# The expert mixture of a fused adaLN block: one fp32 matmul replaced by two fp32r matmuls over split operands

## The chip, the cores and the metric

One Trainium2 chip, one of its cores. The metric is the time of one execution on the device in microseconds (us), the median of several runs. An execution uses five engines that run their own instruction streams and wait for one another by semaphores: PE (TensorE, matmuls), ACT (ScalarE), DVE (VectorE), POOL (GpSimd) and SP (SyncE, which here only issues DMAs).

## The reference

A transformer block with adaptive layer norm, on x of 4 x 512 tokens and 512 features. Its first half is causal attention with 32 heads of 128 (8 key/value heads). Its second half, which the change is in, is a router over 64 experts whose experts are only bias rows:

```
h = _layernorm(x) * (1 + cb) + sb
logits = einsum('th,eh->te', flat, router_weight) + router_bias
scores = softmax(logits)
topk_w, topk_idx = top_k(scores, 8)
w_sum = topk_w.sum(axis=-1, keepdims=True)
w_dense = zeros((T, 64)).at[arange(T)[:, None], topk_idx].add(topk_w)
out = flat * w_sum + einsum('te,eh->th', w_dense, expert_bias)
x = x + gb * out
```

The last einsum is the mixture: for each tile of 128 tokens, a [128 x 64] matrix of weights times the [64 x 512] matrix of expert rows.

## The kernel before, in words

The attention runs as 128 head steps, `t` = 0 to 127. Four steps (h = `t % 4` = 0 to 3, the heads of one key/value group) make a unit `u`, which is one group of one batch row; the units of the first three batch rows come first. Each engine has a `step(t)` of its own in which its work stands in a fixed order written by hand, and the engines meet only through semaphores. Nearly every large matmul of the attention is of the split type: an operand is held as a high part, which ACT makes by copying to fp32r, and a low part, which POOL or DVE makes by subtracting the high part from the original; three fp32r passes (lo x hi, hi x lo, hi x hi) add up in PSUM.

The second half works on 16 tiles of 128 tokens. Tiles 0 to 11 (the first three batch rows) are woven into the steps from `FFN_FROM` = 91 on, one stage of the pipeline in every second step: `ffn_tile(t)` gives n for t = 91, 93, 95, ..., 121, and in that step the engines do for tile n-1 norm, transpose and copy, for n-2 the logits and bias, for n-3 exp, top-8 and weights, and for n-4 the mixture and output. So the weights of tiles 0 to 11 are made in steps 97, 99, ..., 119, and their mixtures in steps 99 to 121. The last four tiles a, b, c, d come after the attention, in the tail, in an order of their own.

Order of a step with an n, as far as the change touches it:

- PE: scores of step t+1, q projection of t+3 (`q_proj`, L467), k or v projection, output projection of t-2 (L564), **mixture of tile n-4** (`ffn_mix`, L596), logits of n-2 (L584), values of t-1 (L549), transpose of h2 for n-1 (L575), **transpose of the weights of n-3** (`ffn_weights_T`, L591). The score matmuls of the next step follow in the queue.
- ACT: `exponentials`, `normalise`, `q_split` (L777: the high part of q for step t+3, which waits for POOL's `rot_c`, L1393), then h2T copy (L830) and **weightT copy** (L844).
- DVE: `ffn_norm`, `q_rope`, `ffn_top` of n-3 (L1186 to L1209, of which L1201 is the `tensor_tensor` of `ffn_choose`), bias of n-2 (L1173), `ffn_out` of n-4 (L1223), then `transpose_blocks(t+1)` (L1088), in steps with h = 1 two `add_out` (L1104), and then, at the head of the next step, `mask_and_max` (L1063 and L1065), which reads the bank of scores `s3` that the next `q_proj` writes.
- POOL: `split_moved_lo` (L1404), `ffn_norm` (L1450, L1452), `q_rope` (L1393), `q_split` (L1398: the low part of q, released by ACT's L777), in h = 0 `k_rope`, then `ffn_out` (L1458, L1460), and in the steps between those with an n also `ffn_stats` and `ffn_gate` (L1426).

PE's queue is strictly in order. `q_proj(t)` begins with `pe.wait_ge(dve_s, score_read(t - 2, 3))`: it may not write bank `s3` before DVE has read the scores of step t-2 out of it.

Of the kernel before, what the change touches and what calls it, by code (L numbers as in the profile page):

```python
# [7 lines left out]
F32 = mybir.dt.float32  # L8
# [106 lines left out]
def build(nc, A, out):  # L115
    ctx = ExitStack()
    with ctx:
# [35 lines left out]
        for at, p in ((wq_at, "hi"), (wq_at + 4 * GROUP * CH * HD, "lo")):  # L153
# [42 lines left out]
        experts = after0.take("experts", [EXPERTS, HID])  # L196
        router = after0.take("router", [P, CH, EXPERTS])
        logit, rest, weight = ([after0.take(f"{n}{i}", [P, EXPERTS]) for i in range(W_RING)]
                               for n in ("logit", "rest", "weight"))
        weightT = [after0.take(f"weightT{i}", [EXPERTS, P]) for i in range(W_RING)]  # L200
# [3 lines left out]
        h2 = [(after1 if i < F_RING - 1 else after2).take(f"h2_{i}", [P, HID]) for i in range(F_RING)]  # L204
        gate1, shift2, scale2, gate2 = [], [], [], []
# [107 lines left out]
        def sem(name):  # L313
# [16 lines left out]
        d_xin, d_xend, d_router = sem("d_xin"), sem("d_xend"), sem("d_router")  # L330
# [32 lines left out]
         out_done) = (sem(f"f_{n}") for n in (  # L363
             "gated", "residual", "x1", "stat", "aggregated", "with_eps", "root", "normed", "scaled", "shifted", "transposed",
             "h2T", "logits", "bias", "minus_max", "exp", "top", "replaced", "chosen", "weighed", "wT", "wT_copy",
             "mix", "mixed", "gated2", "out"))
# [39 lines left out]
        def tensor_program(pe):  # L406
# [172 lines left out]
            def ffn_logits(i, ps):  # L579
                if 0 <= i < TILES:  # L580
                    pe.wait_ge(h2T_copy, i + 1)
                    pe.wait_ge(d_router, 48)
# [141 lines left out]
        def scalar_program(act):  # L724
# [114 lines left out]
            def ffn_weights_copy(i, ps):  # L839
                if 0 <= i < TILES:  # L840
# [3 lines left out]
                    act.activation(weightT[i % W_RING][:], bank[ps][0:EXPERTS, 0:P], ACT.Copy).then_inc(wT_copy, 1)  # L844

            def step(t):
# [98 lines left out]
            ffn_h2T(c, "pv")  # L945
            ffn_weights_copy(a, "s1")
            ffn_exp(b)
            ffn_h2T(d, "pv")
            ffn_weights_copy(b, "s1")
            ffn_exp(c)  # L950
            ffn_weights_copy(c, "s1")
            ffn_exp(d)
            ffn_weights_copy(d, "s1")


        def vector_program(dve):
# [209 lines left out]
            def ffn_bias(i, ps):  # L1166
                if 0 <= i < TILES:
# [4 lines left out]
                    dve.wait_ge(d_router, 48)  # L1172
# [16 lines left out]
            def ffn_replace(i):  # L1189
                if 0 <= i < TILES:  # L1190
                    w = i % W_RING
                    dve.wait_ge(top_done, i + 1)
                    if i >= W_RING:
                        dve.wait_ge(weighed, i - W_RING + 1)
# [8 lines left out]
            def ffn_weigh(i):  # L1203
                if 0 <= i < TILES:
                    s, w = small[i % F_RING], i % W_RING
                    dve.wait_ge(chosen, i + 1)
                    if i >= W_RING:
# [599 lines left out]
```

## Time and profile before

| | |
|---|---|
| median of 3 runs | 1544.13 us (1540.83 to 1544.83) |
| the profiled execution, its own time | 1543.16 us |
| its span, first to last instruction | 1541.7 us |
| what lies around the span | 1.5 us |
| instructions | 24819 |
| mean granted TensorE clock | 0.987 |

The span and all durations below are of the one profiled execution. A busy PE in the profile is an engine whose pipelined matmuls overlap, so the time that a matmul really takes in the queue is read as the distance between starts (its pitch), not as its own duration.

### The profile page before, as it was taken

How to read it: one execution, taken by the hardware profiler on the slowest of the kernel's cores; microseconds unless marked ns; L12 is line 12 of the kernel's file. 1: busy time of each engine (PE TensorE's matmuls, PEld its weight loads, DVE VectorE, ACT ScalarE, POOL GpSimd, SP SyncE). 2: the span in 40 equal slices, each digit the busy share in tenths (PEclk: the TensorE clock that was granted, in tenths of full speed). 3: DMA queues.
4: the chain of work that ended last, by engine and by line, in shares of the span. 5: the costliest groups of instructions: out<-in, count | busy, mean ns of one | idle time of the engine just before them, and what ended most of it. 6: DMA issues, size and time to landing. Idle time of an engine off the chain costs nothing.

```text
span 1541.7 us, 24819 instructions
## 1 busy us (share of the span) xinstructions
PE 1497.7 (97%) x7474; PEld 1262.6 (82%) x7474; DVE 1166.0 (76%) x3441; ACT 969.4 (63%) x2299; POOL 1051.5 (68%) x790
## 2 busy tenths in 40 slices
PE   7979999999999999999999999999999999999977
PEld 4668888888888888888888888888888888888864
DVE  6866777777777777777777777777888889887757
ACT  3356766667667676666766767676666565665651
POOL 1666776776667667677666766766777888876662
PEclk9999999999999999999999999999999999999996
DMA  8547565665665756556566575666778878877640
GB/s 303 214 152 229 188 223 174 198 212 180 203 194 195 215 188 220 173 190 222 175 198 200 190 221 184 217 199 208 232 239 264 260 246 271 265 256 252 214 152 27
DMA packets 209683, 321.60 MB, mean 209 GB/s; under 512 B 37312, under 2 KB 127168, under 8 KB 209552
## 3 DMA queue, kind: packets, MB, share of 16 engines
q1 hardware_dynamic: 209232, 319.93, 64.6%
q8 instruction: 60, 0.98, 0.2%
q14 instruction: 71, 0.58, 0.1%
q10 hardware_dynamic: 320, 0.11, 0.0%
HBM read 179.02 MB, written 140.94 MB: 208 GB/s over the span
## 4 chain that ended last, share of the span: by engine, by line
PE 82%; DVE 4%; POOL 4%; DMA 3%; SPq 3%; issue 2%; ACT 2%; DVEq 0%; POOLq 0%; ACTq 0%
PE bank_s L467 20%; PE bank_o L564 20%; PE bank_pv L549 14%; PE bank_s L514 13%; PE bank_s L490 5%; PE bank_s L478 5%; POOL PT_lo L1404 2%; DMA kv_raw<-vblocks 1%; PE bank_s L446 1%; PE bank_s L584 1%; DMA blocks<-blocks 1%; SPq L1632 1%; PE bank_s L596 1%; SPq L1597 1%; DMA wmod<-in_wmod 1%
## 5 line engine op out<-in xcount | busy, mean ns | idle before, releaser
L1404 POOL TENSOR_TENSOR PT_lo<-PT_raw,PT_hi 128x640 fp32r<-128x640 f32 x254 | 402.0, 1604 | 79.2 <-ACT PT_hi L816 78.9
L802 ACT ACTIVATE probs<-probs,row_inv 128x512 f32<-128x512 f32 (+3 forms) x512 | 258.6, 554 | 171.2 <-DVE row_inv L1071 170.7
L1393 POOL TENSOR_TENSOR rot_c<-rot_c,rot_s 128x512 f32<-128x512 f32 x128 | 165.6, 1294 | 242.8 <-DVE rot_s L1034 242.8
L795 ACT ACTIVATE probs<-probs,row_min 128x512 f32<-128x512 f32 (+3 forms) x512 | 280.5, 551 | 8.1 <-DVE row_min L1065 8.0
L1065 DVE CUSTOM_DVE_ANT_0 probs<-bank_s,mask 128x512 f32<-128x512 f32 (+3 forms) x512 | 231.7, 488 | 1.0 <-issue 0.6
L1398 POOL TENSOR_TENSOR qT_lo<-rot_c,qT_hi 128x512 fp32r<-128x512 f32 x128 | 167.1, 1306 | 92.8 <-ACT qT_hi L777 92.8
L467 PE MATMUL bank_s<-hT_lo,wq_hi 128*128 128x512 f32 x500 | 204.9, 410 | 5.0 <-DVE row_min L1065 2.9
L1088 DVE STREAM_TRANSPOSE blocks<-probs 128x384 f32<-128x384 f32 x508 | 205.1, 442 | 4.2 <-POOL hT_lo L1383 2.1
L564 PE MATMUL bank_o<-wo_lo,OT_hi 128*128 128x512 f32 x504 | 196.3, 389 | 0.9 <-DVE OT_lo L1096 0.9
L564 PE MATMUL bank_o<-wo_hi,OT_lo 128*128 128x512 f32 x504 | 196.1, 389 | 0.0
L564 PE MATMUL bank_o<-wo_hi,OT_hi 128*128 128x512 f32 x504 | 196.1, 389 | 0.0
L467 PE MATMUL bank_s<-hT_hi,wq_hi 128*128 128x512 f32 x500 | 195.2, 390 | 0.0
L467 PE MATMUL bank_s<-hT_hi,wq_lo 128*128 128x512 f32 x500 | 195.0, 390 | 0.0
L816 ACT ACTIVATE PT_hi<-PT_raw 128x640 fp32r<-128x640 f32 x254 | 172.8, 730 | 10.5 <-DMA PT_raw<-blocks 10.0
L549 PE MATMUL bank_pv<-PT_lo,v_hi 128*128 128x512 f32 x508 | 164.5, 324 | 4.6 <-POOL PT_lo L1404 4.6
L514 PE MATMUL bank_s<-kT_lo,qT_hi 128*128 128x512 f32 (+3 forms) x512 | 161.2, 315 | 6.5 <-issue 3.0
L514 PE MATMUL bank_s<-kT_hi,qT_lo 128*128 128x512 f32 (+3 forms) x512 | 165.6, 323 | 0.0
L822 ACT ACTIVATE OT_hi<-bank_pv 128x512 fp32r<-128x512 f32 x126 | 75.4, 598 | 142.4 <-PE bank_pv L549 136.2
L549 PE MATMUL bank_pv<-PT_hi,v_hi 128*128 128x512 f32 x508 | 164.5, 324 | 0.0
L549 PE MATMUL bank_pv<-PT_hi,v_lo 128*128 128x512 f32 x508 | 164.5, 324 | 0.0
L514 PE MATMUL bank_s<-kT_hi,qT_hi 128*128 128x512 f32 (+3 forms) x512 | 164.1, 321 | 0.0
L1063 DVE MEMSET wait_slot<- 128x1 f32 x384 | 22.7, 59 | 166.4 <-PE bank_s L514 166.4
(214 smaller groups left out, 3366.3 us busy)
## 6 DMA issues: line engine op xcount, KB each, us to landing
blocks<-blocks SPq DMA_DIRECT2D x127, 640.0 KB, 4.2
PT_raw<-blocks SPq DMA_DIRECT2D x508, 160.0 KB, 3.1
stage<-in_wq SPq DMA_DIRECT2D x32, 256.0 KB, 4.1
vblocks<-kv_raw SPq DMA_DIRECT2D x32, 256.0 KB, 4.5
kv_raw<-vblocks SPq DMA_DIRECT2D x128, 64.0 KB, 3.2
stage<-in_wo SPq DMA_DIRECT2D x32, 256.0 KB, 4.1
split_wq<-wq_hi SPq DMA_DIRECT2D x32, 256.0 KB, 3.9
split_wq<-wq_lo SPq DMA_DIRECT2D x32, 256.0 KB, 4.5
```

The lines of the kernel that those rows point to most:

```text
L467: mm = pe.matmul(q_bank(t)[:], w[:, h, c, :], x[:, b * CH + c, :], start=(c == 0 and n == 0), stop=(c == CH - 1 and n == 2))
L514: mm = pe.matmul(score_bank[qt], q[:, qt * P:(qt + 1) * P], k[:, 0:(qt + 1) * P], start=(n == 0), stop=(n == 2))
L549: mm = pe.matmul(to, a[:, kb, :], ps, start=(kb == 0 and n == 0), stop=(kb == KEY_ORDER[-1] and n == 2))
L564: mm = pe.matmul(bank[f"o{j}"][:], o[:, j * P:(j + 1) * P], w[:, h, :], start=(h == 0 and n == 0), stop=(t == last and n == 2))
L795: ins = act.activation(row(t, qt), row(t, qt), ACT.Exp, bias=row_min[m][:, qt:qt + 1], scale=-1.0, accum_out=row_sum[m][:, qt:qt + 1])
L802: ins = act.activation(row(t, qt), row(t, qt), ACT.Copy, scale=row_inv[t % 2][:, qt:qt + 1])
L816: act.activation(PT[0][:, at], PT_raw[:, at], ACT.Copy).then_inc(act_t, 1)
L1065: dve.tensor_tensor_reduce(row(t, qt), score_bank[qt], mask[:, SEQ - (qt + 1) * P:], -SCALE, -LOWEST, ALU.add, ALU.min, row_min[m][:, qt:q ...
L1088: ins = dve.transpose(blocks_v[:, qt:qt + 3 * whole_keys - 2:3], keys[:, 0:whole_keys])
L1393: pool.tensor_tensor(rot_c[:], rot_c[:], rot_s[:], ALU.add).then_inc(pool_a, 1)
L1398: pool.tensor_tensor(lo[:], rot_c[:], hi[:].bitcast(F32), ALU.subtract).then_inc(pool_q, 1)
L1404: pool.tensor_tensor(PT[1][:, at], PT_raw[:, at], PT[0][:, at].bitcast(F32), ALU.subtract).then_inc(pool_t, 1)
```

## The change

The mixture's operands become of the split type. Per tile, the weights [128 tokens x 64] are written twice side by side into one [128 x 128] fp32r tile: in columns 0 to 63 their high part (a new ACT copy, `ffn_weights_hi`), in columns 64 to 127 their low part (a new DVE subtraction, `ffn_weights_lo`). Its transpose then has 128 rows, high weights in the upper half and low weights in the lower. The 64 expert rows are loaded twice, into both halves of the 128 rows, and split once into `experts_hi` (ACT) and `experts_lo` (POOL) in step 96. The mixture is two fp32r matmuls of 128 rows, with `experts_lo` and `experts_hi`, in place of one fp32 matmul of 64 rows. `ffn_weigh` now writes into `rest` in place. The expert rows are loaded in step 94 by two DMAs in place of step 88 by one; the router's loads stay. In the tail the DVE order changes by the new subtractions and by `add_bias(d)`, which moves ahead of `ffn_out(b)`.

```diff
@@ tiles @@
+        weight = [after0.take(f"weight{i}", [P, 2 * EXPERTS], F32R) for i in range(W_RING)]
+        weightT = [after0.take(f"weightT{i}", [P, P], F32R) for i in range(W_RING)]
...
+        experts_in = Region(after2.at).take("experts_in", [P, HID])
+        experts = [after2.take(f"experts_{p}", [P, HID], F32R) for p in ("lo", "hi")][::-1]
@@ PE @@
             def ffn_weights_T(i, ps):
-                    pe.wait_ge(weighed, i + 1)
-                    pe.transpose(bank[ps][0:EXPERTS, 0:P], weight[i % W_RING][:], ident[:]).then_inc(wT, 1)
+                    pe.wait_ge(w_lo, i + 1)
+                    pe.transpose(bank[ps][:, 0:P], weight[i % W_RING][:].bitcast(F32), ident[:]).then_inc(wT, 1)
             def ffn_mix(i, ps):
                     pe.wait_ge(wT_copy, i + 1)
-                    pe.matmul(bank[ps][:], weightT[i % W_RING][:], experts[:], start=True, stop=True).then_inc(
+                    if i == 0:
+                        pe.wait_ge(e_lo, 1)
+                    pe.matmul(bank[ps][:], weightT[i % W_RING][:], experts[1][:], start=True, stop=False)
+                    pe.matmul(bank[ps][:], weightT[i % W_RING][:], experts[0][:], start=False, stop=True).then_inc(
                         mix_done, 1)
@@ ACT @@
+            def ffn_weights_hi(i):
+                if 0 <= i < TILES:
+                    w = i % W_RING
+                    act.wait_ge(weighed, i + 1)
+                    if i >= W_RING:
+                        act.wait_ge(wT, i - W_RING + 1)
+                    act.activation(weight[w][:, 0:EXPERTS], rest[w][:], ACT.Copy).then_inc(w_hi, 1)
+
+            def split_experts():
+                act.wait_ge(d_experts, 32)
+                act.activation(experts[0][:], experts_in[:], ACT.Copy).then_inc(e_hi, 1)
...
                 for g, i in pieces(t):
                     split_chunk(g, i)
+                if t == FFN_FROM + 5:
+                    split_experts()
                 if n is not None:
+                    ffn_weights_hi(early(n - 3))
                     ffn_h2T(early(n - 1), "s1")
                     ffn_weights_copy(early(n - 3), "s2")
@@ DVE @@
             def ffn_weigh(i):
-                    dve.tensor_scalar(weight[w][:], rest[w][:], s[:, 7:8], 0.0, ALU.mult, ALU.add,
+                    dve.tensor_scalar(rest[w][:], rest[w][:], s[:, 7:8], 0.0, ALU.mult, ALU.add,
                                       accum_out=s[:, 8:9]).then_inc(weighed, 1)
+
+            def ffn_weights_lo(i):
+                if 0 <= i < TILES:
+                    w = i % W_RING
+                    dve.wait_ge(w_hi, i + 1)
+                    dve.tensor_tensor(weight[w][:, EXPERTS:], rest[w][:], weight[w][:, 0:EXPERTS].bitcast(F32),
+                                      ALU.subtract).then_inc(w_lo, 1)
...
                     ffn_out(early(n - 4), "s1")
+                    ffn_weights_lo(early(n - 3))
                 if moved(t + 1):
                     transpose_blocks(t + 1)
@@ POOL @@
+            def split_experts():
+                pool.wait_ge(e_hi, 1)
+                pool.tensor_tensor(experts[1][:], experts_in[:], experts[0][:].bitcast(F32), ALU.subtract).then_inc(e_lo, 1)
...
                 if t + 1 == FFN_FROM:
                     ffn_gate(0)
+                if t == FFN_FROM + 5:
+                    split_experts()
@@ SP @@
+            def load_experts():
+                sp.wait_ge(pe_qp, GROUP * last_unit(SHARED - 1) + GROUP)
+                for half in range(2):
+                    sp.dma_start(experts_in[half * EXPERTS:(half + 1) * EXPERTS, :], A["eb"]).then_inc(d_experts, 16)
```

The order on DVE in step 101 (tile 2, h = 1) before: `rest` and `top` are the ring buffers of `ffn_top`, `h_1_138` is the tile's output, `blocks` what `transpose_blocks` writes, `y<-bank_o,y` the two `add_out`.

```order
L1201 TENSOR_TENSOR rest_127<-logit_123,rest_127 128x64
L1209 TENSOR_SCALAR weight_131,small_105<-rest_127,small_105 128x64
L1173 ISA logit_124,small_106<-bank_s,router_bias 128x64
L1173 ISA small_106 128x1
L1180 TENSOR_SCALAR small_106<-small_106 128x1
L1223 SCALAR_TENSOR_TENSOR h_1_138<-h_1_138,small_104,bank_s 128x512
L1088 STREAM_TRANSPOSE blocks<-probs 128x3x4x32
```

And of the change at the same place (its lines are some 28 to 33 higher in number):

```order
L1229 TENSOR_TENSOR rest_126<-logit_122,rest_126 128x64
L1235 TENSOR_SCALAR rest_126,small_105<-rest_126,small_105 128x64
L1201 ISA logit_123,small_106<-bank_s,router_bias 128x64
L1201 ISA small_106 128x1
L1208 TENSOR_SCALAR small_106<-small_106 128x1
L1256 SCALAR_TENSOR_TENSOR h_1_137<-h_1_137,small_104,bank_s 128x512
L1242 TENSOR_TENSOR weight_130<-rest_126,weight_130 128x64
L1116 STREAM_TRANSPOSE blocks<-probs 128x3x4x32
```

One instruction is new, the subtraction L1242, between the output of the older tile and the block transposes of the next head; everything of DVE's step that follows stands behind it.

The order on ACT in the same step before, from the last of `normalise` on:

```order
L802 ACTIVATE probs<-probs,row_inv_100 128x128
L777 ACTIVATE qT_hi_81<-rot_c 128x512
L830 ACTIVATE stage_57<-bank_s 128x512
L844 ACTIVATE weightT_135<-bank_s 64x128
L822 ACTIVATE OT_hi<-bank_pv 128x4x4x32
```

And of the change:

```order
L811 ACTIVATE probs<-probs,row_inv_100 128x128
L786 ACTIVATE qT_hi_81<-rot_c 128x512
L861 ACTIVATE weight_130<-rest_126 128x64
L839 ACTIVATE stage_57<-bank_s 128x512
L853 ACTIVATE weightT_134<-bank_s 128x128
L831 ACTIVATE OT_hi<-bank_pv 128x4x4x32
```

The copy L861, for which DVE's subtraction waits, stands behind the copy of q's high part (L777 before, L786 now).

The order on ACT in the tail, for tiles b, c and d, of the change (before, it had the same rows without the three `weight` copies of L861):

```order
L845 ACTIVATE logit_121,small_106<-logit_121,small_106 128x64
L839 ACTIVATE stage_57<-bank_pv 128x512
L861 ACTIVATE weight_129<-rest_125 128x64
L853 ACTIVATE weightT_133<-bank_s 128x128
L845 ACTIVATE logit_122,small_107<-logit_122,small_107 128x64
L861 ACTIVATE weight_130<-rest_126 128x64
L853 ACTIVATE weightT_134<-bank_s 128x128
L845 ACTIVATE logit_123,small_103<-logit_123,small_103 128x64
L861 ACTIVATE weight_131<-rest_127 128x64
```

The exponential of the next tile (L845) stands behind both copies of the tile before it.

## Rows read from the trace of the kernel before

**Rows 1.** The page: PE's busy time, and the granted clock in 40 slices.
```profile
PE 1497.7 (97%) x7474; PEld 1262.6 (82%) x7474; DVE 1166.0 (76%) x3441; ACT 969.4 (63%) x2299; POOL 1051.5 (68%) x790
...
PEclk9999999999999999999999999999999999999996
```

**Rows 2.** Windows: busy us per engine, granted clock, DMA share, GB/s.
```profile
1165.00:1440.00 275.00, 273.47 (x1374) 224.43 (x1372) 232.08 (x701) 168.30 (x421) 213.51 (x166) 1.00 0.80 258
```

**Rows 3.** Chain that ended last, step 109: start us, us, what.
```profile
1290.99 2.72 PE bank_o L564 x12
1293.71 1.05 PE bank_s L596 x2
1294.77 1.03 PE bank_s L584 x8
...
1300.49 2.98 PE bank_s L467 x12
```

**Rows 4.** The tile `weightT`: ns min/median/max, first and last start us.
```profile
L844 ACT ACTIVATE weightT<-bank_s x16: 256/258/272, 1152.6 to 1535.0; 64x128 f32<-64x128 f32 x16
```

**Rows 5.** Timeline of ACT, step 109: start us, us, then idle before it.
```profile
1296.47 0.63 ACT L777 ACTIVATE qT_hi<-rot_c 128x512 fp32r<-128x512 f32 x1 [2.20 <-POOL rot_c L1393]
```

**Rows 6.** Timeline of POOL, steps 97, 101, 107, 109 and 113.
```profile
1144.38 3.29 POOL L1404 TENSOR_TENSOR PT_lo<-PT_raw,PT_hi 128x640 fp32r<-128x640 f32 x2
...
1152.25 1.28 POOL L1398 TENSOR_TENSOR qT_lo<-rot_c,qT_hi 128x512 fp32r<-128x512 f32 x1 [0.74 <-ACT qT_hi L777]
...
1200.20 1.28 POOL L1398 TENSOR_TENSOR qT_lo<-rot_c,qT_hi 128x512 fp32r<-128x512 f32 x1 [0.74 <-ACT qT_hi L777]
...
1272.11 1.29 POOL L1398 TENSOR_TENSOR qT_lo<-rot_c,qT_hi 128x512 fp32r<-128x512 f32 x1 [0.74 <-ACT qT_hi L777]
...
1293.94 1.26 POOL L1452 TENSOR_TENSOR h<-h,shift 128x512 f32<-128x512 f32 x1
...
1297.18 1.28 POOL L1398 TENSOR_TENSOR qT_lo<-rot_c,qT_hi 128x512 fp32r<-128x512 f32 x1 [0.74 <-ACT qT_hi L777]
...
1345.39 1.28 POOL L1398 TENSOR_TENSOR qT_lo<-rot_c,qT_hi 128x512 fp32r<-128x512 f32 x1 [0.74 <-ACT qT_hi L777]
```

**Rows 7.** Timeline of DVE, the same steps, and one row of the tail.
```profile
1149.57 0.58 DVE L1088 STREAM_TRANSPOSE blocks<-probs 128x384 f32<-128x384 f32 x1
...
1199.29 0.57 DVE L1088 STREAM_TRANSPOSE blocks<-probs 128x384 f32<-128x384 f32 x1
...
1272.54 0.57 DVE L1088 STREAM_TRANSPOSE blocks<-probs 128x384 f32<-128x384 f32 x1
...
1274.85 0.06 DVE L1063 MEMSET wait_slot<- 128x1 f32 x1 [0.56 <-PE bank_s L514]
...
1293.98 1.30 DVE L1201 TENSOR_TENSOR rest<-logit,rest 128x64 f32<-128x64 f32 x1
...
1296.85 0.57 DVE L1088 STREAM_TRANSPOSE blocks<-probs 128x384 f32<-128x384 f32 x1
...
1300.31 0.08 DVE L1065 DVE_READ_ACCUMULATOR2_ANT row_min<- 128x1 f32 x1
...
1345.62 0.57 DVE L1088 STREAM_TRANSPOSE blocks<-probs 128x384 f32<-128x384 f32 x1
...
1519.47 0.22 DVE L1201 TENSOR_TENSOR rest<-logit,rest 128x64 f32<-128x64 f32 x1
```

**Rows 8.** Waits of SP's DMA queue, 1165 to 1440: us, times, longest.
```profile
SPq L1628 <- POOL PT_lo L1404: 86.8, 23, 5.9
```

**Rows 9.** Chain that ended last, in the tail.
```profile
1522.83 2.00 PE bank_o L596 x2
...
1532.87 1.29 DVE rest L1201
...
1537.47 0.76 DVE h L1223
```

**Rows 10.** Windows: a stretch behind a wait of PE.
```profile
1486.00:1491.00 5.00, 4.28 (x19) 4.05 (x20) 0.17 (x1) 2.16 (x6) 4.84 (x5) 0.66 0.66 161
```

More of the change, by code:

```diff
@@ L195, in build @@
         after0 = Region(lo_start)
-        experts = after0.take("experts", [EXPERTS, HID])
         router = after0.take("router", [P, CH, EXPERTS])
-        logit, rest, weight = ([after0.take(f"{n}{i}", [P, EXPERTS]) for i in range(W_RING)]
-                               for n in ("logit", "rest", "weight"))
-        weightT = [after0.take(f"weightT{i}", [EXPERTS, P]) for i in range(W_RING)]
+        logit, rest = ([after0.take(f"{n}{i}", [P, EXPERTS]) for i in range(W_RING)] for n in ("logit", "rest"))
+        weight = [after0.take(f"weight{i}", [P, 2 * EXPERTS], F32R) for i in range(W_RING)]
+        weightT = [after0.take(f"weightT{i}", [P, P], F32R) for i in range(W_RING)]
         assert after0.at <= lo_start + hT_bytes
@@ L362, in build @@
          bias, minus_max, exp_done, top_done, replaced, chosen, weighed, wT, wT_copy, mix_done, mixed, gated2,
-         out_done) = (sem(f"f_{n}") for n in (
+         out_done, e_hi, e_lo, w_hi, w_lo) = (sem(f"f_{n}") for n in (
              "gated", "residual", "x1", "stat", "aggregated", "with_eps", "root", "normed", "scaled", "shifted", "transposed",
              "h2T", "logits", "bias", "minus_max", "exp", "top", "replaced", "chosen", "weighed", "wT", "wT_copy",
-             "mix", "mixed", "gated2", "out"))
+             "mix", "mixed", "gated2", "out", "e_hi", "e_lo", "w_hi",
+             "w_lo"))
         dve_end = sem("dve_end")
@@ L581, in ffn_logits @@
                     pe.wait_ge(h2T_copy, i + 1)
-                    pe.wait_ge(d_router, 48)
+                    pe.wait_ge(d_router, 32)
                     for c in range(CH):
@@ L843, in ffn_weights_copy @@
                         act.wait_ge(mix_done, i - W_RING + 1)
-                    act.activation(weightT[i % W_RING][:], bank[ps][0:EXPERTS, 0:P], ACT.Copy).then_inc(wT_copy, 1)
+                    act.activation(weightT[i % W_RING][:], bank[ps][:, 0:P], ACT.Copy).then_inc(wT_copy, 1)
+            def ffn_weights_hi(i):
[8 more added lines that the diff above has]
+                act.activation(experts[0][:], experts_in[:], ACT.Copy).then_inc(e_hi, 1)
             def step(t):
@@ L945, in scalar_program @@
             ffn_h2T(c, "pv")
+            ffn_weights_hi(a)
             ffn_weights_copy(a, "s1")
@@ L948, in scalar_program @@
             ffn_h2T(d, "pv")
+            ffn_weights_hi(b)
             ffn_weights_copy(b, "s1")
             ffn_exp(c)
+            ffn_weights_hi(c)
             ffn_weights_copy(c, "s1")
             ffn_exp(d)
+            ffn_weights_hi(d)
             ffn_weights_copy(d, "s1")
@@ L1358, in vector_program @@
             add_bias(b)
+            ffn_weights_lo(a)
             begin(d)
@@ L1362, in vector_program @@
             add_bias(c)
+            ffn_weights_lo(b)
             ffn_out(a, "o0")
             ffn_top(c)
+            add_bias(d)
+            ffn_weights_lo(c)
             ffn_out(b, "o1")
-            add_bias(d)
             ffn_top(d)
+            ffn_weights_lo(d)
             ffn_out(c, "o2", whole=True)
@@ L1641, in load_rows, with load_router @@
                     sp.dma_start(to[:], mod_d[n, b:b + 1, :].broadcast_to([P, HID])).then_inc(d_rows[b], 16)
-            def load_experts():
+            def load_router():
                 sp.wait_ge(pe_qp, GROUP * last_unit(0) + GROUP)
-                sp.dma_start(experts[:], A["eb"]).then_inc(d_router, 16)
                 sp.dma_start(router[:], A["rw"]).then_inc(d_router, 16)
                 sp.dma_start(router_bias[:], A["rb"].broadcast_to([P, EXPERTS])).then_inc(d_router, 16)
+            def load_experts():
+                sp.wait_ge(pe_qp, GROUP * last_unit(SHARED - 1) + GROUP)
+                for half in range(2):
+                    sp.dma_start(experts_in[half * EXPERTS:(half + 1) * EXPERTS, :], A["eb"]).then_inc(d_experts, 16)
             def ffn_load(i):
@@ L1740, in sync_program @@
                 if t + 3 == FFN_FROM:
+                    load_router()
+                if t == FFN_FROM + 3:
                     load_experts()
```

9 lines of the change are left out of this document (4 added, 5 removed).

## The prediction

> **What bounds the kernel now.** I read the page first. PE is busy for 97% of the span at the full clock in 39 of 40 slices [rows 1]; the reader is to see that whatever PE's queue loses or saves in the steps is lost or saved in the end, unless another engine holds PE up. Then the windows of the stretch in which the early tiles' mixtures lie, 1165 to 1440 us: PE 273.5 of 275 us, but DVE 232 and POOL 213.5 of them [rows 2]. So PE bounds here by a small margin, and the question is where the other two touch it. The chain of waits through step 109 shows what PE does with its time there: twelve output-projection matmuls, the mixture, the logits, values, transposes, the next scores, and then `q_proj` [rows 3]. Last, the timelines of POOL, ACT and DVE around the place where the change puts its two new instructions, step for step.
>
> One spot in them carries the prediction. In step 109 DVE has no idle time from its transposes on (1296.85, [rows 7]) through the two `add_out` to the mask of the highest query block, whose last piece starts at 1300.31 and takes 0.08. PE's `q_proj`, which must not write bank `s3` before that, starts at 1300.49 [rows 3]. So there DVE, not PE, sets the start: what delays DVE's transposes in such a step delays PE one for one. In the steps with h = 3 there are no `add_out`, and DVE instead waits for PE: 0.56 us before the mask in step 107 [rows 7].
>
> **What PE saves.** The mixture takes 1.05 us of the queue, start to next start 1.06 [rows 3]. The twelve 512-column fp32r matmuls before it take 2.72, or 0.227 each [rows 3]. Two of them are 0.45: saved 0.60 per tile, for twelve early tiles 7.2 us if nothing takes it back. The transpose of 128 instead of 64 columns of weights moves the same 128 columns, and I cost it at nothing beside the pass before it; the bound is the 0.1 that a score matmul waits for a larger weight load, 1.2 us in all.
> By the Trainium skill (FP8 and Floating Point Precision, TensorE Precision Notes) a true fp32 matmul is four passes. Four passes at 0.227 would be 0.91, so by it the saving would be 0.45 per tile and 5.4 us in all; the trace has 1.05 for the pair, and I take the trace.
>
> **What the two new instructions add.** Both are short. ACT's copy of 64 columns: I take 0.25, as the weightT copy has it [rows 4]. DVE's subtraction is a `tensor_tensor` of 128x64 with both inputs in SBUF, of the same form as L1201: that took 0.22 in the tail with POOL idle, and 1.30 in step 109, where it started at 1293.98, 0.04 behind a POOL operation of 1293.94 to 1295.20, and ended 0.08 after that [rows 6, 7]. So it costs 0.22 with POOL idle, and otherwise it ends about 0.09 after the POOL instruction that it met.
> The Trainium skill (SBUF — State Buffer, Who interferes with whom) says the same: a DVE instruction with two SBUF inputs and a GpSimd instruction that reads SBUF shut each other out for their whole length. It speaks against this change, whose new subtraction is of that form and stands where POOL is at work.
>
> **When they can run.** ACT's copy stands behind `q_split`, which ends at 1297.10 in step 109 because it waited for POOL's `rot_c` [rows 5]. The end of the same `q_split` releases POOL's `qT_lo`, 1297.18 to 1298.46 [rows 6]. The high part is there at 1297.10 + 0.25 = 1297.35, the subtraction finds POOL just started, and ends at 1298.46 + 0.09 = 1298.55. DVE's transposes started at 1296.85 [rows 7]: they are now 1.70 later, and with them the `add_out`, the mask and `q_proj`. PE's earlier arrival by 0.60 is worth nothing there, since POOL's and ACT's times hang on the q projection at the head of the step, before the mixture.
>
> The same rule, end of `qT_lo` plus 0.09 minus start of the transposes, gives the other steps:
> - h = 1, steps 101, 105, 109, 113: first 1200.20 + 1.28 + 0.09 - 1199.29 = 2.3, last 1345.39 + 1.28 + 0.09 - 1345.62 = 1.1 [rows 6, 7], between them 1.9 and 1.7. Sum **+7.0**, PE's saving already spent.
> - h = 1, steps 117 and 121: in 117 `qT_lo` has ended before DVE comes, DVE's chain begins with the logits and so gains a part of the 0.60; in 121 there is a mixture but no subtraction. I take -0.3 each, **-0.6**.
> - h = 3, steps 99 to 119: in step 107 DVE comes 1272.11 + 1.29 + 0.09 - 1272.54 = 0.95 later [rows 6, 7]. Of it the 0.56 of idle time goes first [rows 7], and the mask then has some 0.4 before PE asks for its bank: PE loses and gains nothing. The six steps lie between -0.6 (subtraction early, saving kept) and +0.45 (step 119); sum **-0.7**.
> - Step 97, tile 0: there is no `ffn_out` yet, so DVE came to its transposes at 1149.57, far ahead of `qT_lo`, which ended at 1153.53 [rows 6, 7]: 4.05. POOL's share of splitting the experts (one 128x512 operation, 1.3 as `qT_lo`'s) stands right before its `PT_lo` of 1144.38 [rows 6], in a row of POOL work without gaps up to `rot_c`, so it moves `qT_lo` by 1.3 as well: 5.35. Before, the mask had 1.0 to spare there and PE 0.1 of its own, less what the larger lateness uses up: **+4.5**.
>
> ACT's one split of the experts (0.6) lies in idle time of ACT before its next work from PE, at nothing, at most 0.6 once. SP issues one DMA more and six steps later; SP waits for POOL for 86.8 us in 23 steps [rows 8], so its issues are covered; uncovered, they would delay by the issue of two DMAs, once. Block stores go out later with the transposes, up to 2.3 us, but PE is later by as much, so the transfers keep their lead; in h = 3 steps at most 1 us of it is used.
>
> **The tail.** The mixtures run at half clock there, 2.00 us each [rows 9]; as two passes at 2 x 0.227 each about 0.9. Against it, each tile's weights now go DVE, ACT, DVE, PE, ACT, PE with two more hand-overs, some 0.25 + 0.22 + 0.15 = 0.6, DVE waits for ACT while the next tile's work stands behind, and the exponential of tile d stands behind the copies of c. For the last tile I have the subtraction kept off by the POOL operation that now meets L1201 for 1.29 [rows 9], so that one delay moves from one instruction to the other. Worked through to the end: weights of d 0.5 later, mixture of d done 0.6 earlier (1536.9 where `ffn_out` of d started at 1537.47, [rows 9]), but DVE first ends `ffn_out` of c at 1537.3. Last instruction -0.2; I take **0**, with -1 to +2.
>
> **The sum.** 7.0 - 0.6 - 0.7 + 4.5 + 0 = +10.2 on the profiled execution's 1543.16, so 1553.4. The median of the runs shown is 1.0 above that execution, so 1554.3, and I say 1554. A difference under 0.3% (4.6 us) is about what these runs can't tell from none.
>
> **Rivals.**
> - *The subtraction does not collide.* If it slips in for 0.22 whatever POOL does, it ends some 0.9 earlier in the steps that wait for ACT: about 0.9 x 5 in h = 1 and in step 97 and 2 in h = 3, and the sum is +3 to +4: 1548. Against it is L1201, which ended with POOL's operation in step 109 [rows 6, 7]. Chance 0.12.
> - *PE keeps its saving (other side: faster).* The place is `q_proj` behind the mask. If DVE's lateness was taken up before it, PE would keep 7.2 of saving less the waits for the transposed weights alone; from an average DVE delay under about 0.5 us on, the change gains. The delays from rows are 1.1 to 2.3 in the h = 1 steps, so this needs ACT's copy to come before `q_split`, which the order excludes. With 4.5 for tile 0 left it gives 1541, with nothing left 1537. Chance 0.08.
> - *More is lost.* PE's pauses in step 97 add up to over 4 us within two steps. After a pause of that size, before 1486, the granted clock was 0.66 for 5 us [rows 10]. That is 1.7 us more for the first tile, and a backlog of POOL or DVE that outlives a step may add 0.5 for each of six tiles; 1559. Chance 0.2.
> - *The forecast's case*, 1551 to 1557: chance 0.6.
>
> **The numbers.** The first and last are the unknown sizes: the low end takes in the first rival (1547), the high end the third (1561). Faster 0.08, same (1539.5 to 1548.7) 0.14, slower 0.78.
>
> **What would show it.** In the changed trace: two mixture matmuls with starts 0.23 apart; `weight` L1242 of DVE with about 1.1 to 1.3 us in most early steps and its end just after `qT_lo`; DVE waiting for ACT's L861 before it; PE idle before `q_proj` in steps 101, 105, 109, 113 by 1.1 to 2.3 and about 4.5 lost in step 97; a span of the stretch from step 101 to 121 longer by about 6. The prediction is wrong if L1242 takes 0.22 throughout, or if PE's time per two steps falls by 0.6 in h = 1 steps.

## The result, and the profile after

The changed kernel takes 1552.05 us (median of 5 runs, 1550.27 to 1552.53), the one before 1544.13 in the runs beside it: a ratio of 1.0051, 95% interval 1.0039 to 1.0062. That is 7.9 us more; forecast were 10. The profiled execution took 1550.27 us with a span of 1549.0, 7.3 more than the span of before.

The page of the changed kernel, its first line of busy times and the granted clock in 40 slices:

```profile
PE 1488.3 (96%) x7474; PEld 1267.9 (82%) x7474; DVE 1175.5 (76%) x3457; ACT 973.5 (63%) x2316; POOL 1052.2 (68%) x791
...
PEclk9999999999999999999999999999999999999996
```

Against [rows 1], PE works 9 us less in a span that is 7 us longer: PE got its saving, and stands still for more than it. The page's 40 slices do not show where; for that one has to go to the instructions.

The tiles of the change, from the views of `weight` and `weightT` (ns min/median/max, first and last start):

```profile
L861 ACT ACTIVATE weight<-rest x16: 237/241/257, 1153.2 to 1541.6; 128x64 fp32r<-128x64 f32 x16
L1242 DVE TENSOR_TENSOR weight<-rest,weight x16: 224/950/1262, 1153.5 to 1541.9; 128x64 fp32r<-128x64 f32 x16
...
L604 PE MATMUL bank_s<-experts_lo,weightT x12: 389/389/389, 1177.0 to 1447.1; 128*128 128x512 f32 x12
L605 PE MATMUL bank_s<-experts_hi,weightT x12: 389/389/389, 1177.2 to 1447.4; 128*128 128x512 f32 x12
```

L604 and L605 start 0.23 us apart, and the pair of them takes the place of the 1.05 us in [rows 3]. The subtraction L1242 takes 0.22 at its shortest (in the tail, with POOL idle) and 1.26 at its longest.

Step 101 on the timelines of the changed kernel. DVE, from the output of the older tile on (the bracket is idle time and who ended it):

```profile
1202.66 0.75 DVE L1256 SCALAR_TENSOR_TENSOR h<-h,small,bank_s 128x512 f32<-128x512 f32 x1
1204.08 1.24 DVE L1242 TENSOR_TENSOR weight<-rest,weight 128x64 fp32r<-128x64 f32 x1 [0.67 <-ACT weight L861]
1205.24 0.56 DVE L1116 STREAM_TRANSPOSE blocks<-probs 128x384 f32<-128x384 f32 x1
...
1206.91 1.25 DVE L1132 TENSOR_TENSOR y<-bank_o,y 128x512 f32<-128x512 f32 x2
1208.09 0.68 DVE L1093 CUSTOM_DVE_ANT_0 probs<-bank_s,mask 128x512 f32<-128x512 f32 x1
...
1208.70 0.08 DVE L1093 DVE_READ_ACCUMULATOR2_ANT row_min<- 128x1 f32 x1
```

POOL and ACT at the same time:

```profile
1203.98 1.26 POOL L1436 TENSOR_TENSOR qT_lo<-rot_c,qT_hi 128x512 fp32r<-128x512 f32 x1 [0.74 <-ACT qT_hi L786]
```

```profile
1203.27 0.64 ACT L786 ACTIVATE qT_hi<-rot_c 128x512 fp32r<-128x512 f32 x1 [2.05 <-POOL rot_c L1431]
1203.80 0.24 ACT L861 ACTIVATE weight<-rest 128x64 fp32r<-128x64 f32 x1
```

And PE:

```profile
1205.47 0.30 PE L597 MATMUL bank_s<-ident,weight 128*128 128x128 f32 x1 [1.00 <-DVE weight L1242]
...
1207.42 0.27 PE L520 MATMUL bank_s<-kT_hi,qT_hi 128*128 128x128 f32 x1
1208.88 0.47 PE L473 MATMUL bank_s<-hT_lo,wq_hi 128*128 128x512 f32 x1 [1.19 <-issue]
```

DVE is done at 1203.41 and waits 0.67 for ACT's copy, which stands behind `qT_hi`. The same end of `qT_hi` has let POOL start at 1203.98. DVE comes at 1204.08, is kept off until POOL's operation ends at 1205.24, and ends at 1205.32. PE waits 1.00 for the weights, and then 1.19 more before `q_proj`, which starts 0.10 after the mask's end at 1208.78. Since the mask sets that start, PE would be no earlier without the first wait; e8 takes the first one away.

To see where time goes, take the start of the first matmul of `q_proj` in each step from PE's timeline, of both kernels, and add up by how much the distance from one step to the next has grown. A step's number stands for the stretch from its own `q_proj` to the next one. From step 95 to 124:

| us, against the kernel before | forecast | changed | changed again (e11) |
|---|---|---|---|
| steps 96 to 98 (tile 0, split of the experts) | +4.5 | +6.3 | +4.6 |
| h = 1: 101, 105, 109, 113 | +7.0 | +5.7 | +6.9 |
| h = 3: 99, 103, ..., 119 | -0.7 | -2.0 | -2.3 |
| 117, 120, 121 | -0.6 | -1.5 | -1.6 |
| all other steps from 95 | 0 | +0.4 | +0.4 |
| tail, from `q_proj` of 124 on | 0 | -0.5 | +0.7 |

Single executions also differ ahead of step 95, before the first new instruction of a tile: by 0.1 to 1.2 us, in e7 by 2.2. The table leaves that out; it is what separates its sums from the spans.

### The profile page after: what moved, and what is told of

It reads as the page before. It is cut to its first block, busy times and chain, and to the rows that moved or that the text cites. A ratio compares the mean times of both kernels' runs of the same rounds, so it can differ in the third digit from the quotient of the medians.

```text
span 1549.0 us, 24854 instructions
## 1 busy us (share of the span) xinstructions
PE 1488.3 (96%) x7474; PEld 1267.9 (82%) x7474; DVE 1175.5 (76%) x3457; ACT 973.5 (63%) x2316; POOL 1052.2 (68%) x791
## 4 chain that ended last, share of the span: by engine, by line
PE 72%; DVE 9%; POOL 8%; issue 4%; DMA 3%; SPq 3%; ACT 2%; DVEq 0%; POOLq 0%; ACTq 0%
PE bank_s L473 18%; PE bank_o L570 18%; PE bank_pv L555 12%; PE bank_s L520 12%; PE bank_s L496 5%; PE bank_s L484 4%; POOL PT_lo L1442 2%; POOL rot_c L1431 1%; DMA blocks<-blocks 1%; DMA kv_raw<-vblocks 1%; PE bank_s L452 1%; SPq L1641 1%; DMA wmod<-in_wmod 1%; POOL qT_lo L1436 1%; DVE blocks L1116 1%
```

## The experiments

Ratios are to the kernel before on the same chip, as recorded with their 95% intervals; times in us are those ratios times 1544.1. They are not exactly the ratios of the two medians, which differ from them by up to 0.0007 (1 us). "Steps" are sums as in the table above, from one profiled execution each.

**e1, the saving alone.** The weights are not split (their low part is left out), the expert rows are; two fp32r passes over 64 rows.

```diff
-                    ffn_weights_hi(early(n - 3))
-                    ffn_weights_lo(early(n - 3))
...
-                    pe.wait_ge(w_lo, i + 1)
+                    pe.wait_ge(weighed, i + 1)
...
+                    pe.matmul(bank[ps][:], weightT[i % W_RING][0:EXPERTS, :], experts[1][0:EXPERTS, :], start=True, stop=False)
```

> The mixture as two fp32r passes over 64 rows, with the expert rows split into high and low part, but the weights not split: no high copy on ACT, no subtraction on DVE, and the low part of the weights is left out of the result. It shows the saving without its price. By the theory on record (DVE bounds the steps with h = 1 at the mask, PE the ones with h = 3) PE keeps 0.6 us in each of the six h = 3 steps and some 0.3 to 0.6 after the mixtures of steps 117, 119 and 121, nothing in the h = 1 steps 101 to 113, and loses about 1.3 to 1.5 in step 97 to POOL's split of the experts: 3 to 4 us below the kernel before. The rival that PE's saving counts in every step gives 6 to 7 below; the rival that fp32r passes save nothing here gives +1.

Measured 1540.1, ratio 0.9975 (0.9963 to 0.9987), -3.9. The number is what the theory on record had; how it comes about is not, so it is no proof of the theory. The profiled execution, the slowest of the ten and 5.8 above their median, has the h = 3 steps at -2.3. Three of the four h = 1 steps gain 0.35 to 0.38, where nothing was expected; the fourth (105) loses 1.3, in a stretch of lower clock (last section). In the steps with h = 0, of which no theory spoke, it loses 6.1. e7 takes that up.

**e2, the price alone.** Everything of the change but the two passes; one fp32 matmul over the high parts (the low parts are left out).

```diff
-                    pe.matmul(bank[ps][:], weightT[i % W_RING][:], experts[1][:], start=True, stop=False)
-                    pe.matmul(bank[ps][:], weightT[i % W_RING][:], experts[0][:], start=False, stop=True).then_inc(
+                    pe.matmul(bank[ps][:], weightT[i % W_RING][0:EXPERTS, :].bitcast(F32),
+                              experts[0][0:EXPERTS, :].bitcast(F32), start=True, stop=True).then_inc(
```

> The changed kernel with its high copy, its subtraction, its waits and its split of the experts, but the mixture itself is one fp32 matmul over the 64 rows of the high parts; the low parts are left out of the result. It shows the price without the saving. If prices and saving add step by step as the theory has it, it is slower than the changed kernel by 0.6 us in each h = 3 step and in the last three mixtures, not in the h = 1 steps, where DVE bounds: 4 to 5 us above the changed kernel, so 12 to 13 above the one before. If the fp32r mixture or its larger weight loads were what cost time, this kernel would be as fast as the one before or within 2 us of it.

Measured 1555.74, ratio 1.0079 (1.0061 to 1.0096), +12.2 by the ratio; the two medians differ by 11.6. The h = 1 steps cost 5.6, as in the changed kernel (5.7): there PE's saving is worth nothing. The h = 3 steps cost 0.5 where the changed kernel gains 2.0. So the price is the hand-over and not the new matmuls.

**e3, no collision.** The second instruction of DVE reads one SBUF tile and writes zeros in place of the low part (left out); all waits stay.

```diff
-                    dve.tensor_tensor(weight[w][:, EXPERTS:], rest[w][:], weight[w][:, 0:EXPERTS].bitcast(F32),
-                                      ALU.subtract).then_inc(w_lo, 1)
+                    dve.tensor_scalar(weight[w][:, EXPERTS:], rest[w][:], 0.0, 0.0, ALU.mult, ALU.add,
+                                      accum_out=spare[:]).then_inc(w_lo, 1)
```

> The changed kernel, but DVE's second instruction is a tensor_scalar with accumulator that reads one SBUF tile and writes zeros in place of the low part (which is left out of the result); it waits for the same copy of ACT and PE waits for it. In the trace before that form took 0.28 whatever POOL did. If the loss comes from DVE shutting POOL out and being shut out (collision), the subtraction's 1.24 us becomes about 0.3 and the h = 1 steps lose 0.4 in place of 1.2 to 1.8: total 4 to 5 us below the changed kernel. If the wait for ACT's copy is what costs and the collision doesn't, it stays within 1 us of the changed kernel.

Measured 1545.06, ratio 1.0007 (0.9997 to 1.0016). The view of `weight` in that run:

```profile
L1243 DVE TENSOR_SCALAR_CACHE_REDUCE weight<-rest x16: 209/219/222, 1155.4 to 1537.6; 128x64 fp32r<-128x64 f32 x16
```

Though it starts beside POOL's `qT_lo` as before, that instruction never takes over 0.22. The kernel is 6.8 below the changed one (1.0007 against 1.0051); expected were 4 to 5. The h = 3 steps are at -4.4 and keep nearly all of PE's saving. The h = 1 steps are still at +3.2 (0.2, 0.8, 1.0 and 1.3, where 0.4 each was expected): in 109 and 113 DVE waits 1.62 and 1.81 for ACT's copy, in place of 0.68 and 0.67. So without the collision most of the net loss is gone, but in the h = 1 steps the wait for ACT alone still costs.

**e4, the wait for ACT taken away.** The high copy goes ahead of `qT_hi` in ACT's queue.

```diff
+                if n is not None:
+                    ffn_weights_hi(early(n - 3))
                 if t + 3 < ALL:
                     q_split(t + 3)
...
                 if n is not None:
-                    ffn_weights_hi(early(n - 3))
                     ffn_h2T(early(n - 1), "s1")
```

> The changed kernel with ACT's high copy ahead of the copy of q's high part in its queue, so that DVE no longer waits for ACT behind POOL, and DVE comes to its subtraction while POOL waits for ACT between rot_c and qT_lo in steps 105 and 109. Theory: steps 105 and 109 lose 0.3 in place of 1.8 and 1.3, 101 about 0.4, 113 still about 1.2 since qT_lo has begun there, step 97 about 2 in place of 5.5; the h = 3 steps as before: 6 to 8 us below the changed kernel, within 2 us of the kernel before. The rival that PE's own wait for the transposed weights, or the larger transpose, costs the time gives less than 2 us.

Measured 1545.16, ratio 1.001 (1.0001 to 1.002), 6.3 below the changed kernel. From step 101 on, the h = 1 steps lose 0.23, 0.28, 0.25 and 0.27, steps 96 to 98 together 1.3. The sizes of 105 and 109 are as expected, but not their cause: the subtraction did not slip in before `qT_lo`. It met the POOL operation before it, `rot_c`, in all four h = 1 steps and took 1.08 to 1.14, as here in step 101:

```profile
1200.12 1.09 DVE L1243 TENSOR_TENSOR weight<-rest,weight 128x64 fp32r<-128x64 f32 x1
```

```profile
1199.86 1.28 POOL L1432 TENSOR_TENSOR rot_c<-rot_c,rot_s 128x512 f32<-128x512 f32 x1
```

Only four of its twelve runs in the steps (103, 107, 111 and 119) took 0.22. So e3 has the wait without the collision, and e4 has the collision without the wait. For the four h = 1 steps together, with e7 below as the case that has neither:

| us, h = 1 steps 101 to 113 | no collision on DVE | collision |
|---|---|---|
| no wait for ACT behind `qT_hi` | -3.0 (e7) | +1.0 (e4) |
| wait | +3.2 (e3) | +5.7 and +6.9 (changed) |

By these single executions the collision costs 1.0 a step by itself, the wait 1.6, and the two together 2.2 to 2.5. The wait is the larger part there. The kernels differ in more than these two things (e7 has the experts' split later and the subtraction on POOL), so the split is an estimate.

**e5, the experts split later.** POOL's operation goes from the end of step 96 into its idle time in step 98.

```diff
                     k_split(u + 1)
+                if t == FFN_FROM + 7:
+                    split_experts()
...
-                if t == FFN_FROM + 5:
-                    split_experts()
```

> The changed kernel with POOL's part of splitting the experts moved from the end of step 96 to step 98, where POOL was idle before rot_c (nothing is left out). If that one operation of 1.3 us was passed on in step 97, the increment there (5.5 us) falls by about 1.3, and the kernel is 1 to 1.5 us below the changed one. If step 97 is long only because DVE waits for ACT, it stays within 0.3 of the changed one.

Measured 1550.71, ratio 1.0042 (1.0025 to 1.0059), 1.4 below the changed kernel's 1.0051, though the intervals overlap. The trace is clearer: step 97 costs 3.1, against 4.4 and 4.2 in the two executions of the changed kernel. POOL's 1.3 us were passed on.

**e6 and e7, the low part on POOL.** The high copy as in e4; POOL subtracts between `rot_c` and `qT_lo`, where it had waited 0.74 for ACT [rows 6]. e7 is e6 with the edit of e5. Nothing is left out.

```diff
+            def ffn_weights_lo(i):
+                if 0 <= i < TILES:
+                    w = i % W_RING
+                    pool.wait_ge(w_hi, i + 1)
+                    pool.tensor_tensor(weight[w][:, EXPERTS:], rest[w][:], weight[w][:, 0:EXPERTS].bitcast(F32),
+                                       ALU.subtract).then_inc(w_lo, 1)
...
                 if t + 3 < ALL:
                     q_rope(t + 3)
+                if n is not None:
+                    ffn_weights_lo(early(n - 3))
+                if t + 3 < ALL:
                     q_split(t + 3)
```

> The high copy ahead of q's on ACT, and in the steps the low part subtracted by POOL in place of DVE, between rot_c and qT_lo, where POOL waited 0.74 us for ACT before; in the tail as in the changed kernel (nothing is left out). DVE's row is then as before the change. Theory: h = 1 steps 101 to 113 lose nothing, h = 3 steps and the last mixtures keep 0.6, step 97 loses 1.3 to 1.5 for the experts: 3 to 4 us below the kernel before, as in the run without split weights. If the subtraction costs where it runs whatever the engine (POOL's row is full from PT_lo to rot_c), it loses 0.3 in each of twelve steps and ends at the time before.

> Both edits, the low part on POOL and the experts split in step 98 (nothing is left out). If the parts add up, 1.3 us below the one with only the low part on POOL: about 4.5 to 5 us below the kernel before.

Measured 1543.03 for e6, ratio 0.9982 (0.9973 to 0.9991), and 1540.6 for e7, 0.9976 (0.9964 to 0.9987): -2.8 and -3.7. Both are faster than both kernels of the case, and both a little less so than expected; their intervals overlap, so that e7 beats e6 is not shown. The subtraction does what it should; from the view of `weight` in e7:

```profile
L1484 POOL TENSOR_TENSOR weight<-rest,weight x12: 311/322/331, 1150.9 to 1414.1; 128x64 fp32r<-128x64 f32 x12
```

Now all four h = 1 steps gain, 0.73 to 0.77 each, which the theory had excluded; the h = 3 steps gain 4.5 together. But the h = 0 steps give 5.2 back. What is late there is named by the waits between 1165 and 1440 us, first of e7 and then of the kernel before (total us, times, longest):

```profile
ACT v_hi L798 <- DMA kv_raw<-vblocks: 22.0, 6, 4.8
```

```profile
ACT v_hi L789 <- DMA kv_raw<-vblocks: 12.6, 6, 3.3
```

and by SP's timeline in e7, step 99:

```profile
1169.90 2.82 SPq L1686 DMA_DIRECT2D PT_raw<-blocks  x4
1172.82 0.38 SPq L1658 DMA_DIRECT2D wo_hi<-split_wo  x1
...
1175.13 0.43 SPq L1658 DMA_DIRECT2D wv_lo<-split_wv  x1
1175.61 1.90 SPq L1677 DMA_DIRECT2D kv_raw<-vblocks  x4
```

The values of the next unit come back through memory, and their loads are issued behind six weight loads. ACT's `v_hi` waited for them before the change too. When PE is early, `v_hi`, the exponentials behind it, then rope and masks, are not: so the gain would be given back one step later. e9 tests that.

**e8, DVE's lateness alone.** e7, and DVE does a subtraction of the same form into a spare tile, at the place and with the wait of the changed kernel; nobody waits for it.

```diff
+            def stand_in(t, i):
+                if 0 <= i < TILES:
+                    w = i % W_RING
+                    dve.wait_ge(w_hi, i + 1)
+                    dve.wait_ge(act_q, t + 4)
+                    dve.tensor_tensor(spare[:], rest[w][:], weight[w][:, 0:EXPERTS].bitcast(F32),
+                                      ALU.subtract)
```

> The same as the last, but DVE runs an idle subtraction of the same form into a spare tile at the place where the changed kernel has its own, and waits there for the end of ACT's copy of q's high part; nobody waits for it, and PE gets the weights early. It tells DVE's lateness from PE's own wait for the transposed weights. If the loss goes through DVE (mask, then q_proj), the h = 1 steps lose 1.2 to 1.8 again, the h = 3 steps keep most of their 0.6, and the kernel is 8 to 10 us above the one without the stand-in, 4 to 5 above the kernel before. If it goes through PE's wait for the weights, it is within 1 us of the one without the stand-in.

Measured 1559.92, ratio 1.0099 (1.0081 to 1.0118). It tells the two ways apart as it should: PE has its weights early, and yet the h = 1 steps 101 to 113 lose 0.9 to 1.3 each. The loss goes through DVE, the mask and `q_proj`. But it is 19 above e7, twice what was expected, and slower than the changed kernel. Two things were not foreseen. The h = 3 steps keep nothing of their saving (+0.4 together, where e7 has -4.5): there the stand-in starts 0.02 to 0.05 behind `qT_lo` and takes 1.3. And the step after each h = 1 step loses too: 102, 106, 110, 114 and 118 lose 1.6 each, 8.1 in all, where the changed kernel loses 0.4. The windows of that run, around `q_proj` of step 102 (the last number but two is the granted clock), say why:

```profile
1206.00:1208.50 2.50, 2.44 (x15) 1.81 (x13) 2.50 (x7) 2.27 (x5) 2.42 (x3) 1.00 1.01 361
1210.00:1215.00 5.00, 4.80 (x14) 3.88 (x15) 4.93 (x18) 2.84 (x10) 3.87 (x3) 0.66 0.62 205
```

PE waited 1.72 in one piece before `q_proj`, at 1208.5 to 1210.2, and the clock then fell to its lower level for a part of the next 5 us; the twelve matmuls of `q_proj` took 4.57 there and 2.96 in the step before. The four other steps have waits of 1.76 to 2.07, and a `q_proj` of 4.52 to 4.59. In the changed kernel's step 101 the delay comes as 1.00 and 1.19 with matmuls between, and the clock stayed at 1.00.

**e9 and e10, the values' loads first.** On SP, in steps with h = 3, the loads of the values go ahead of the weight loads: e9 on top of e7, e10 on the kernel before. Nothing is left out.

```diff
-                for name, u in again(t):
-                    load_split(name, u)
                 u, h = t // GROUP, t % GROUP
+                if h == 3 and u + 1 < UNITS:
+                    load_values(u + 1)
+                for name, v_unit in again(t):
+                    load_split(name, v_unit)
                 if h == 2 and u + 1 < UNITS:
                     store_values(u + 1)
-                if h == 3 and u + 1 < UNITS:
-                    load_values(u + 1)
```

> The kernel with the low part on POOL and the experts split later, and on SP the four loads of the values (kv_raw) moved ahead of the loads of split weights in the steps with h = 3 (nothing is left out). In the run without it the gains of the h = 1 and h = 3 steps are given back by 5.2 us in the four h = 0 steps and before 117, where the chain goes from those loads (issued behind six weight loads, landing after 5.0 us) to ACT's v_hi. If the loads' place in SP's queue is what is late, they are issued 2.7 us earlier and 3 to 5 us come back: 7 to 9 us below the kernel before. If the transfer itself is slow because the DMA engines are full, at most 1 us comes back.

> The kernel before, with only SP's order changed in the same way (nothing is left out). Before the change PE bounded the h = 0 steps and the values were in time, so if the theory of the gain given back holds, this alone is worth nothing in the mixture's steps: within 1 us of the kernel before; anything it gains in the last steps, whose chain holds the same loads, must be taken off the result of the other.

Measured 1536.07 for e9, ratio 0.9951 (0.9937 to 0.9965), -7.6: the fastest of all. e10 1541.81, ratio 0.9981 (0.9971 to 0.999), -2.9, where at most 1 had been expected. In e9's trace the loads are issued at 1170.94 and have landed at 1175.24, where e7 has 1175.61 and 1182.08. ACT's `v_hi` no longer waits for them, the h = 0 steps give back nothing (-0.1 instead of +5.2), and the four h = 1 steps keep their 0.8 each:

```profile
1170.94 1.85 SPq L1677 DMA_DIRECT2D kv_raw<-vblocks  x4
1172.89 0.38 SPq L1658 DMA_DIRECT2D wo_hi<-split_wo  x1
```

Not all is gain: e9's step 117 loses 1.4 (PE waits 1.37 for the transposed weights and 1.29 before `q_proj`) and 121 loses 0.3, where e7 gains 0.8 and 0.6. Why was not followed up.

In e10's trace the h = 0 steps are unchanged (0.0), so there the values had cost PE nothing; it gains 1.0 in steps 96 to 98 and 0.6 in 120. Its profiled execution is 1.5 above its median and no faster than the profiled one of the kernel before, so the rest of its 2.9 is not located. By the ratios, e7's 3.7 and e10's 2.9 add up to 6.6 of e9's 7.6, and only 1 is left for the two together; by the steps 95 to 123 of the traces it is 3.4. Which of the two is right stays open; that the giving back in the h = 0 steps ends with the loads' place is what the trace shows.

**e11, the changed kernel again.**

> The changed kernel unchanged, on the same chip as the two others. The first result gave a ratio of 1.0051 to the kernel before; the same is expected, 1.004 to 1.006, and in its trace the same steps: 97 with the largest loss, 101 to 113 with h = 1 at 1.2 to 1.8 each, and a granted clock under 1.0 after step 97's wait.

Measured 1551.91, ratio 1.0047 (1.0034 to 1.006). Its steps are in the table above. The h = 1 steps lie between 1.3 and 2.4. The highest, 109, is above what was expected: PE waited 1.84 for the transposed weights there, and the clock fell behind it:

```profile
1305.30:1310.30 5.00, 5.00 (x19) 4.43 (x20) 5.00 (x20) 3.70 (x9) 4.92 (x4) 0.66 0.96 356
```

## Why the prediction was right, point by point

- **Sign and size.** Forecast +10, measured +7.9, within the range; the case that was called the likeliest is the one that happened, with its place (L1242 behind ACT's copy and POOL's `qT_lo`, mask, `q_proj`). e3 and e4 each take one link of it away, and e8 puts the chain back into a faster kernel; each time the h = 1 steps follow, though not by the amounts expected. That the sum comes so near is in part luck: below, the terms are off by up to 2 us and partly cancel.
- **The saving on PE.** 0.60 per mixture: the h = 3 steps of e7 gain 0.76 to 0.80 up to 115, somewhat more than that. The term was small by some 0.2, not by its kind. The mixture itself is 0.60 shorter as forecast (1.06 from its start to the next before, 0.46 in e7). The rest lies at its borders: the fp32 mixture started 0.31 behind the last output projection and the fp32r one 0.22, and the eight logits matmuls behind it took 0.91 and now 0.81. Nothing shows that the larger weight loads cost anything.
- **The price of the subtraction.** 0.22 free and "POOL's end + 0.09" otherwise: seven of the twelve in the steps took 1.24 to 1.26 and one 1.12, having begun within 0.3 behind the start of `qT_lo`; the four others came later into the same operation and took 0.55 to 0.78. All twelve end 0.08 after `qT_lo`. The Trainium skill (SBUF — State Buffer, Who interferes with whom) says that a DVE instruction with two SBUF inputs contends with a GpSimd instruction that reads SBUF, and that one with at most one SBUF input, outside the two-port modes, does not. The traces agree: all twelve were held up until `qT_lo` ended, and e3's form with one input never was.
- **h = 1 steps.** +7.0 forecast, +5.7 and +6.9 measured. Step 101 was sized 2.3 and came to 1.34 and 1.5: POOL's row had been late in that step in the trace before, and now reaches `qT_lo` 0.8 earlier in the step. That this is owed to PE's pause in step 97 is likely but not shown. I had carried the step's distances over unchanged. The nearness of 6.9 to 7.0 is luck: it holds the 2.4 of step 109, which includes a spell of lower clock that the forecast did not have.
- **h = 3 steps and the last ones.** -0.7 and -0.6 forecast, -2.0 and -1.5 measured. The saving of 0.8 in place of 0.6 gives some 1.2 of the difference in the h = 3 steps. The delay was sized too large besides: in step 107 DVE's transposes come 0.5 later in the step and not 0.95, since `qT_lo` ends 0.3 earlier in it. In 117 the -0.3 came true by luck: `qT_lo` had not ended as forecast, the subtraction met it and took 0.55, and the larger saving paid for that. Step 121 gains 0.6 and not 0.3; the half had no row behind it. Another 0.6 is gained in step 120, for which nothing was forecast. It is not PE's saving, since e2 and e10 have the same 0.6 there without any; its cause stays open.
- **Step 97.** +4.5 forecast, +6.3 and +4.6 measured with its neighbours, +4.4 and +4.2 for step 97 alone. The terms were there (DVE's wait, POOL's 1.3); what I left in a rival, the clock, came about in both executions. Windows of the changed kernel, behind PE's wait of 2.74:

```profile
1150.00:1155.00 5.00, 1.85 (x15) 1.44 (x13) 1.54 (x2) 1.26 (x3) 3.80 (x4) 0.86 1.01 288
1155.00:1158.40 3.40, 3.40 (x13) 3.11 (x12) 3.40 (x12) 2.21 (x5) 1.60 (x2) 0.50 0.95 377
1158.50:1163.00 4.50, 4.50 (x18) 3.64 (x18) 4.43 (x15) 2.85 (x10) 2.76 (x2) 0.79 0.50 145
```

  The clock is at 1.2 GHz (0.50) for the scores behind the wait. What shows of it is in step 98, whose `q_proj` takes 3.87 in place of 2.97 (3.27 in e11): +0.9 and +0.3, less than the 1.7 of the rival. The scores themselves run slowly within step 97, which comes to no more than the forecast; that DVE covers them there is argued, not shown. The last 1.0 of the +6.3 is in step 96, before tile 0 has cost anything: PE waits 1.14 there at 1141.25, and ACT's `v_hi` had waited 3.95 for the loads of the values, 1.0 longer than in the kernel before and 0.9 longer than in e11, which has only 0.1 in that step.
- **The tail.** 0 forecast, -0.5 and +0.7 measured; e10, whose tail is that of the kernel before, has +0.8, so no more than that can be read from single executions. The chain there, of the changed kernel, shows the hand-overs added and the mixture shortened from 2.00 [rows 9] to 1.2:

```profile
1541.59 0.27 ACT weight L861
1541.88 0.66 DVE weight L1242
1542.54 0.14 issue
1542.67 0.46 PE bank_s L597
...
1543.49 0.79 PE bank_o L604
1544.28 0.44 PE bank_o L605
1544.75 0.76 DVE h L1256
```

  The granted clock is 0.50 in this stretch. The two passes take 1.20 to 1.23 there, not the 0.9 that I had from 2 x 0.227 each: the second starts 0.57 to 0.59 behind the first, not 0.45, and its own 0.63 to the end counts in full.
- **The rivals.** That the subtraction slips in between fell with the first row of L1242. "PE keeps its saving" fell as far as this order of instructions goes. But its point of decision was right: with a DVE delay near zero (e7, e9) the change gains. The prediction also held that PE's earlier arrival "is worth nothing" in the h = 1 steps. That is true only while DVE's time there is fixed by ACT and POOL. In e7 and e9 those steps gain 0.73 to 0.81, since DVE itself had waited for the logits behind the mixture, and comes earlier with them. The third rival, more lost by the clock, came about in its mechanism (step 97, and 109 in e11), but with 0.3 to 0.9 for tile 0 in place of 1.7.

## What to carry to other kernels

Splitting an operand moves work from the matmul engine to three others, and its price is set by where the two short instructions stand in their queues, not by how long they are: here 0.24 and 0.22 us of work cost 1.2 to 2.4 us in a step with h = 1, and nothing that showed when the copy went ahead of the long wait and the subtraction to the engine that was idle just then. Moving the copy alone (e4) took most of the loss away, although the subtraction still met POOL. Before adding an instruction with two SBUF inputs on VectorE, look at what GpSimd is doing at that very point, above all when both are released by the same event. And when a gain is given back one step later, look for the transfer that was just in time before.

## What the runs showed of the hardware that I had not expected

A single wait of PE in a row of steps where it was otherwise busy can be followed by the lower clock, and the price is then in the matmuls behind it. In e8 five waits of 1.72 to 2.07 us were; the granted clock over the 5 us behind the first was 0.66, and `q_proj` took 1.6 longer each time. So was a wait of 1.84 in e11 (0.66 over 5 us).

These runs give no rule from the length of the wait, though. In e3 a wait of 1.73, with another of 1.20 some 2 us of matmuls later, left the clock at 1.00. So did two waits of 1.00 and 1.19 in the changed kernel. But in e1 two waits of 1.16 and 1.14, with 1.4 us of matmuls between, were followed by the lower clock, and step 105 lost 1.3 by it. The windows behind the waits, first of e3 and then of e1:

```profile
1155.80:1160.80 5.00, 3.80 (x20) 3.31 (x21) 5.00 (x20) 3.75 (x10) 3.90 (x3) 1.00 0.94 360
```

```profile
1243.00:1248.00 5.00, 5.00 (x15) 4.01 (x16) 2.67 (x11) 3.44 (x10) 4.98 (x4) 0.67 0.67 229
```

So whether a delay comes in one piece or in two does not decide it by itself, and what does stays open.
